# A dense network over pairwise products on one core: the last chunk's second layer as seven block products, and five smaller edits

## The reference

```python
interaction = jnp.einsum('bnd,bmd->bnm', bottom_output, bottom_output)
x = jnp.concatenate([bottom_mlp_output, interaction[:, _TRIL_R, _TRIL_C], zero_pad], axis=1)
x = jax.nn.relu(x @ W0.T + b0)
x = jax.nn.relu(x @ W1.T + b1)
x = jax.nn.relu(x @ W2.T + b2)
x = jax.nn.relu(x @ W3.T + b3)
return x @ W4.T + b4
```

## Time and profile before

| | us |
|---|---|
| median of 3 runs | 484.64 (484.17 to 485.58) |
| the profiled execution | 484.05 |
| its span, first to last instruction | 482.3 |
| PE busy | 470.3 |
| PEld busy | 399.2 |
| DVE busy | 282.8 |
| ACT busy | 242.6 |

### The profile page before, as it was taken

How to read it: one execution, slowest core, us unless ns; L and a number is a source line. 1 busy time by engine, 2 the same in 40 slices (tenths; PEclk the granted TensorE clock), 3 DMA queues, 4 the chain that set the end, 5 groups by cost and what they waited for, 6 DMA issues and landing times.

```text
span 482.3 us, 6717 instructions
## 1 busy us (share of the span) xinstructions
PE 470.3 (98%) x2495; PEld 399.2 (83%) x2495; DVE 282.8 (59%) x508; ACT 242.6 (50%) x580; POOL 0.7 (0%) x6
## 2 busy tenths in 40 slices
PE   8989999999997999999999999999999999999997
PEld 8979987878775888888888888888888888888885
DVE  4599779687765877575616877766624633110124
ACT  4996577758673366565653266665553321110112
POOL 0000000000000000000000000000000000000000
PEclk9999999999998999999999999999999999999999
DMA  8979555765273231843345141653224000434200
GB/s 306 379 253 390 175 163 187 253 218 190 87 270 139 85 101 39 307 150 134 103 183 212 44 141 37 219 222 130 87 96 167 1 0 1 175 101 161 87 1 1
DMA packets 18992, 72.28 MB, mean 150 GB/s; under 512 B 2448, under 2 KB 4496, under 8 KB 14864
## 3 DMA queue, kind: packets, MB, share of 16 engines
q1 hardware_dynamic: 18960, 71.86, 42.3%
HBM read 63.45 MB, written 8.40 MB: 149 GB/s over the span
## 4 chain that ended last, share of the span: by engine, by line
PE 82%; DVE 9%; DMA 4%; ACT 2%; issue 2%; SPq 0%; DVEq 0%; ACTq 0%
PE work L790 18%; PE work L792 17%; PE work L791 17%; PE gps L815 8%; PE acc L790 7%; PE acc L791 6%; PE acc L792 6%; DMA xraw<-x_t 4%; DVE turned L605 2%; ACT grams L416 1%; PE acc L912 1%; DVE turned L594 1%; PE gps L828 1%; DVE w1s L662 1%; DVE pairs L609 1%
## 5 line engine op out<-in xcount | busy, mean ns | idle before, releaser
L416 ACT ACTIVATE grams<-gps 32x216 f32<-32x216 f32 x384 | 131.5, 343 | 86.0 <-PE gps L815 82.5
L790 PE MATMUL work<-h1h,w1s 128*128 128x512 f32 x256 | 101.7, 397 | 0.5 <-DVE w1s L662 0.4
L792 PE MATMUL work<-h1l,w1s 128*128 128x512 f32 x256 | 100.4, 392 | 0.0
L791 PE MATMUL work<-h1h,w1s 128*128 128x512 f32 x256 | 100.2, 391 | 0.0
L448 ACT ACTIVATE act_out<-work,bias 128x512 f32<-128x512 f32 (+1 forms) x64 | 42.3, 662 | 90.9 <-PE work L792 89.6
L815 PEld LDWEIGHTS gps<-xs 128*128 128x128 f32 x384 | 56.6, 190 | 10.0 <-issue 1.4
L636 DVE CAST h2h<-act_out 128x512 fp32r<-128x512 f32 x40 | 17.0, 426 | 76.5 <-ACT act_out L448 76.5
L815 PE MATMUL gps<-xs 128*128 128x224 f32 x384 | 58.3, 274 | 0.4 <-DVE featL L627 0.3
L790 PE MATMUL work<-featH,w0l 126*128 126x512 f32 (+5 forms) x160 | 56.7, 354 | 1.1 <-ACT act_out L448 0.6
L792 PEld LDWEIGHTS work<-h1l,w1s 128*128 128x128 f32 x256 | 48.1, 188 | 10.6
L790 PEld LDWEIGHTS work<-h1h,w1s 128*128 128x128 f32 x256 | 48.3, 189 | 9.3 <-DVE w1s L662 1.4
(11 more groups left out here) (71 smaller groups left out, 520.5 us busy)
## 6 DMA issues: line engine op xcount, KB each, us to landing
xraw<-x_t SPq DMA_DIRECT2D x64, 432.0 KB, 4.2
w1s<-w_parts SPq DMA_DIRECT2D x24, 1024.0 KB, 4.8
w_parts<-w1s SPq DMA_DIRECT2D x8, 1024.0 KB, 4.8
stage<-w_t SPq DMA_DIRECT2D x8, 512.0 KB, 5.9
w0raw<-w_t SPq DMA_DIRECT2D x4, 512.0 KB, 8.0
w2raw<-w_t SPq DMA_DIRECT2D x4, 512.0 KB, 9.0
x0raw<-x_t SPq DMA_DIRECT2D x4, 256.0 KB, 5.3
w3raw<-w_t SPq DMA_DIRECT2D x1, 512.0 KB, 10.5
```

Of the source, the lines that this page charges most:

```text
L416: last = act.activation(grams2[rows, h // 2 % 2, at:at + HALF_GROUPS, :, :], src[:, :, :, q * EVEN:q * EVEN + INPUTS], ACT.Copy)
L790: pe.matmul(dst, wl, ah, start=start, stop=False)
L791: pe.matmul(dst, wh, ah, start=False, stop=False)
L792: return pe.matmul(dst, wh, al, start=False, stop=stop)
```

## The change

- **Layer 1 of the last chunk.** The weights and activations are cut in halves both ways, and tiles i and 4+i of the output (a "set", i from 0 to 3) come from seven block products P1 to P7 of 4 products each, 256 samples wide, in place of 16 products of 512 samples. ACT copies P1 out of PSUM, and DVE adds the blocks up in seven sums of 256 columns (U2, U4, C11, U3, C22, C21, C12); a block's bank is free for a later block once its sum is done. DVE also makes the operands: four sums of weights for each set (512 columns each, `s_sum`) with their parts (`s_hi_part` on ACT, `s_lo_part` on DVE, 1024 columns), and four differences of activations for each pair of layer 0 tiles (256 columns each, `t_sum`) with theirs (`t1_lo_part`, `t_lo_part`, `late_parts`). Set 0's weight sums stand at the end of chunk 2. Layer 0's tiles come in the order 0, 4, 1, 5, 2, 6, 3, 7.
- **Narrower grams.** The gram matmuls load 123 weight columns in place of 128.
- **Wide layer 4.** Weights are one column of `w4s`, the moving operand is 512 samples: 6 matmuls a chunk. DVE adds the bias to one row of 512, and each chunk's answers are stored by a DMA of their own.
- **Shifted opening.** Turns after slices 7, 11, 15; weight loads after slices 6, 8, 10, 12. Chunk 0's halves start at steps 2, 6, 10, 14, 19, so that half 5 stands at step 22, half 11 at 42, half 19 at 68, half 27 at 94, half 31 at 106, the turns at 40, 66, 92 and 117.
- **High parts from PSUM.** `relu` writes the high part straight from PSUM on ACT, ahead of `act_out`; DVE's cast is gone.

```diff
-        plans = [plan([3, 8, 13, 18, 23], 2, STEPS - 2)] + [plan([1], 3, STEPS - 6)] * (CHUNKS - 2) + [({}, {})]
+        plans = [plan([2, 6, 10, 14, 19], 2, STEPS - 3)] + [plan([1], 3, STEPS - 6)] * (CHUNKS - 2) + [({}, {})]
-        W0_AFTER = [5, 7, 8, 10]
+        W0_AFTER = [6, 8, 10, 12]
-        TRANSPOSE_AT = SLICES_SUB + 2
+        TRANSPOSE_AT = SLICES_SUB + 3
+        S_SUM_AT = {107: 0, 108: 1, 109: 2, 110: 3}
+        S_PART_AT = {110: 0, 111: 1}
...
+                act.activation(hi[:, kept_cols], bank[:, kept_cols], ACT.Relu, bias=bias[:, row:row + 1])\
+                   .then_inc(hi_done, 1)
                 act.activation(act_out[:, slot(layer, m, more), cols], bank[:, cols], ACT.Relu,
                                bias=bias[:, row:row + 1]).then_inc(relu_done, 1)
...
+                dve.wait_ge(hi_done, n + 1)
                 dve.wait_ge(relu_done, n + 1)
-                dve.tensor_copy(hi, full).then_inc(hi_done, 1)
-                dve.wait_ge(hi_done, n + 1)
                 dve.tensor_tensor(lo, full, hi.bitcast(f32), ALU.subtract).then_inc(split_done, 1)
...
+                def last_layers():
+                    for k in range(1, KQ):
+                        last_even(k)
+                        if k == 2:
+                            answers(c - 1)
+                            s_sum(1, 0)
+                            s_sum(1, 1)
+                        if k == KQ - 1:
+                            s_sum(1, 2)
+                            s_sum(1, 3)
+                        last_odd(k)
+                    for i in range(SETS):
...
+                        if i + 1 < SETS:
+                            s_lo_part(i + 1, 0)
+                        set_sum(i, "U2")
+                        set_sum(i, "U4")
+                        if i + 1 < SETS:
+                            s_lo_part(i + 1, 1)
+                        set_sum(i, "C11")
...
-                                     xs[:, p % XSLOTS, 0, four, :].rearrange("p b n -> p (b n)"),
+                                     xs[:, p % XSLOTS, 0, four, :].rearrange("p b n -> p (b n)")[:, 0:USED],
...
+            def block(i, name, weights, moving):
+                for k in range(KQ):
+                    last = product(place(name), *weights(k), *moving(k), k == 0, k == KQ - 1)
+                last.then_inc(block_done, 1)
...
+            def layers_last():
+                for i in range(SETS):
+                    p1(i)
+                    p5(i)
+                    if i:
+                        layer2_last(2 * i - 2)
+                    p6(i)
+                    p2(i)
+                    if 0 < i < SETS - 1:
+                        layer2_last(2 * i - 1)
+                    p7(i)
+                    p4(i)
+                    p3(i)
+                for pos in range(KT2 - 3, KT2):
+                    layer2_last(pos)
...
-                    for part, (h2, ready) in enumerate(((h2h, hi_done), (h2l, split_done))):
-                        pe.wait_ge(ready, n + 1)
-                        for s in range(SUBS):
-                            at = ((s * MT3 + k) * 2 + part) * 2
-                            last = pe.matmul(acc[:, 3, at:at + 2], h2[:, k, s * SUB:(s + 1) * SUB], w4s[:, k, :],
-                                             start=True, stop=True)
+                    n, whole = nth(c, 3, k, more), acc[0:1, 3, :]
+                    pe.wait_ge(hi_done, n + 1)
+                    pe.matmul(whole, w4s[:, k, 1:2], h2h[:, k, :], start=k == 0, stop=False)
+                    pe.matmul(whole, w4s[:, k, 0:1], h2h[:, k, :], start=False, stop=False)
+                    pe.wait_ge(split_done, n + 1)
+                    last = pe.matmul(whole, w4s[:, k, 0:1], h2l[:, k, :], start=False, stop=k == MT3 - 1)
```

More of the change, by code:

```diff
@@ L20 @@
 GCOLS = GROUP * EVEN
+USED = (GROUP - 1) * QUAD + INPUTS
 BANK = 512
@@ L42 @@
 TILES = MT0 + MT1 + MT2 + MT3
+SETS = MT1 // 2
+HALF = CHUNK // 2
+KQ = KT1 // 2
+WQ = KQ * P
+L0_ORDER = [t for i in range(SETS) for t in (i, SETS + i)]
+L1_ORDER = [t for i in range(SETS) for t in (SETS + i, i)]
+BLOCKS = ("P1", "P5", "P6", "P2", "P7", "P4", "P3")
+SUMS = ("U2", "U4", "C11", "U3", "C22", "C21", "C12")
 LOAD = 1024
@@ L172, in by_sample, with nth_block, nth_sum, place @@
             return buf[:, p % XSLOTS, :].rearrange("p (b n) -> p b n", n=INPUTS)
+        def nth_block(i, name):
+            return len(BLOCKS) * i + BLOCKS.index(name) + 1
+        def nth_sum(i, name):
+            return len(SUMS) * i + SUMS.index(name) + 1
+        def place(name):
+            bank = {"P1": gps[:, 0, :], "P7": gps[:, 0, :], "P5": work[:, 0, :], "P6": gps[:, 1, :], "P4": gps[:, 1, :],
+                    "P2": work[:, 1, :], "P3": work[:, 1, :]}[name]
+            return bank[:, 0:HALF]
+        def tiles(c, layer, m, more=True):
+            return nth(c, layer, m, more) + 1 - (MT1 if c == LAST and layer >= 2 else 0)
+        def tile0(c, m):
+            return L0_ORDER[m] if c == LAST else m
+        def split_columns(c, layer, m):
+            if c == LAST and layer == 0 and m % 2 == 0:
+                return LEFT
+            return columns(c) if layer == 0 else slice(0, CHUNK)
         def w0_piece(buf, n):
@@ L369, in body @@
                         load_x(c + 1, p)
+                if c == LAST:
+                    load_a22(0)
+                    load_raw(1)
+                    answer(c - 1)
+                    for i in range(2, SETS):
+                        load_raw(i)
+                        refill_set(i)
+                        load_a22(i - 1)
+                    load_a22(SETS - 1)
+                    return
+                if c == LAST - 1:
+                    load_raw(0)
                 for m in range(MT1):
+                    if c and m == 2:
+                        answer(c - 1)
                     if c == 0:
@@ L506, in on_tile @@
                 def on_tile(layer, m):
-                    relu(c, layer, m, work[:, m % 2, :])
+                    relu(c, layer, m, work[:, m % 2, :], h1h[:, tile0(c, m), :] if layer == 0 else h2h[:, m % 2, :])
                 def after_tile(m):
@@ new lines, in set_sum @@
+            def set_sum(i, name):
+                first, second = act_out[:, 1, :], act_out[:, 0, :]
+                left, right = slice(0, HALF), slice(HALF, CHUNK)
+                dst, block, part = {"U2": (U2, "P6", P1_OUT), "U4": (U4, "P5", U2), "C11": (first[:, left], "P2", P1_OUT),
+                                    "U3": (U3, "P7", U2), "C22": (second[:, right], "P5", U3),
+                                    "C21": (second[:, left], "P4", U3), "C12": (first[:, right], "P3", U4)}[name]
+                dve.wait_ge(block_done, nth_block(i, block))
+                if name == "U2":
+                    dve.wait_ge(copy_done, i + 1)
+                else:
+                    dve.wait_ge(sum_done, nth_sum(i, name) - 1)
+                dve.tensor_tensor(dst, place(block), part, ALU.add).then_inc(sum_done, 1)
@@ L949, in body @@
                         layer4(c - 1, True)
-                for m in range(MT1):
+                for m in range(MT1 if c < LAST else 0):
                     for k in range(KT1):
```

329 lines of the change are left out of this document (288 added, 41 removed).

## The result

The changed kernel takes 490.6 us (489.92 to 491.15) for 484.7 of the kernel before beside it: ratio 1.0122, 95% interval 1.0098 to 1.0147. It is slower, and 4.0 us outside the forecast range.

What follows compares the result with a forecast made beforehand. The prediction took TensorE as the bound almost everywhere. Its terms summed to -1.3 us, from 484.05 to 482.75, which goes to 483.3 against the median of 484.64; it wrote 483.4, range 480.0 to 486.6.

Steps and rivals of the forecast that it cites:

- a step costs 0.687: TensorE's price in us of one step, with 512-column matmuls starting 0.229 apart, taken from the earlier trace.
- 192 x 0.229: Last chunk's layers 1 and 2: 44.0 us of 512-column matmuls become 336 x 0.118 = 39.8, so -4.1.
- Rival 1: Clock falls in new waits at chunk 2's end and P1: 485.1 with one (chance 0.14), 486.8 with both (0.10).
- Opening: -1.8: Start of the kernel: shorter slice load and overlapping pieces bring the fourth transposes about 1.8 us earlier.
- The lower bound: Opening's gain was bounded between 0 and -2.6 us; the bound meant is 0, no gain.
- Chunk 0: Steps 0 to 23 +0.7 us, steps 24 to 115 +2.6, its end -4.5 with a wait of 0.8.
- my 1.85 and 1.25: Chunk 0: waits in us forecast at the first and second turn, with ACT and DVE behind.
- Grams: Gram matmuls: loads of 123 columns 0.1086 us apart in place of 0.113, -1.0 us, bounds 0 and 2.3.
- End of chunk 2: New wait of 2.6 us ahead of layer 2's last tile, behind four weight sums and two low parts.
- Last chunk's layers 1 and 2: +0.7 us: matmuls save 4.1, set 0 waits 4.8 (P1 2.45, P6 1.7, P3 0.6), sets 1 to 3 none.
- Layer 4 and the tail: Layer 4 -1.2 us, 0.4 in each of three chunks; tail +0.6, up to +1 if the store is dearer.
- the sum of -1.3: All terms together, opening to tail: -1.3 us, from 484.05 to 482.75.

Runs made afterwards that it cites:

- e5: Changed kernel with 96 more bytes ahead of TensorE's moving tiles, so they start 64 over a multiple of 128 as before: 486.75 us, ratio 1.0038.
- e2: Kernel before with 32 bytes left free ahead of xraw, putting moving tiles 96 bytes over a multiple of 128: 488.9 us, ratio 1.0086.
- e6: Kernel before with the shifted opening alone: its loads, transposes, VectorE order and half points: 485.5 us, ratio 1.0008.
- e8: e5 with the last chunk's preparations reordered, set 0's weight sums behind the first pair's low part: 480.3 us, ratio 0.9916.
- e12: e8 with the grams' loads 128 columns wide again in place of 123: 481.75 us, ratio 0.9928.
- e3: e1 with set 0's four weight sums moved from the end of chunk 2 into the last chunk, behind the first pair's low part: 484.2 us, ratio 0.9989.
- e11: e8 with layer 4, answers and store of the kernel before: 480.3 us, ratio 0.9899.
- e7: Kernel before with one edit, high parts made by a second ReLU on ScalarE in place of VectorE's cast: 486.7 us, ratio 1.0036.
- e1: Changed kernel with a 32-byte pad that puts the moving tiles at a multiple of 128: 487.4 us, ratio 1.0044.
- e4: Kernel before with weights 32 bytes over a multiple of 128 and moving tiles at a multiple: 487.8 us, ratio 1.0053.

## Why the prediction was wrong, point by point

- **The step that failed is the price of a matmul.** "a step costs 0.687" and "192 x 0.229" took the pitch from the earlier trace rows into a layout in which it is 3.1 to 4.1 ns more in layer 1. I looked at what the diff does to queues and never at where its new tiles push the old ones. The missing term is +4.1 us (e5 against after; e2, from the other side, has 4.2); less it the measured time would be 486.5, at the very edge of the range, the other misses below making up the rest.
- **Rival 1 came true once**: the fall at 375.0 behind a wait of 2.4. In the sum that is +1.7. P1's 2.1 brought none. With the missing term alone, rival 1's 485.1 becomes 489.2.
- **Opening: -1.8 was 0.** The left half began 1.5 us sooner, but the fourth transposes on VectorE did not come earlier with it: they start at 39.59 for 39.62, and the splits of the left half stand behind them. So TensorE waits 0.94 and 0.30 at 42.6 and 46.5, and step 0 is at 52.61 for 52.63. The lower bound that I had written down held; e6 confirms it.
- **Chunk 0**: steps 0 to 23 +1.4 for +1.2, and step 24 on -1.7 for -2.5, of which 0.3 is the place (e8, without a fall too, has 86.2 for 86.5). The waits of 1.33 and 1.80 behind the first and second turn answer to my 1.85 and 1.25. At the end of the chunk the wait is 0.62 and the clock 1.00, as forecast, but the sum of the chunk's waits is unchanged (5.9 for 5.8), and that the clock did not fall behind the 1.80 is partly luck: e5's did.
- **Grams: right in size.** 0.6 to 1.5 us between e8 and e12 for 1.0. Loads are 106 to 107 ns apart for 108.6, but those of 128 columns were 109.3 and not 113 in chunks 1 and 2: only 0.8 us stand in the grams themselves, and the rest in the matmuls right behind each half, which the term did not have.
- **End of chunk 2: right** in place, releaser and nearly size, 2.4 for 2.6 (e3 and e8 remove it by moving the sums that I named).
- **Last chunk's layers 1 and 2: right.** -1.9 for -1.8; P1 2.1, P6 1.4 and P3 none for 2.45, 1.7 and 0.6; sets 1 to 3 without waits. The seven products are worth what was said; e8 shows that the cost of set 0 was one of order alone.
- **Layer 4 and the tail**: -0.3 a chunk for -0.4, and the tail +1.5 for +0.6, since the answers' single row takes 1.10 us and not 0.69, and the last matmul waits 0.9 for a low part that ends later. e11, with both undone, takes the same time as e8.

Of the 7.2 us between the sum of -1.3 and the 5.9 measured, 4.1 are the place, 1.7 the clock, 1.8 the opening, 0.9 the tail; the shorter waits at the end of chunk 2 and at P1, P6 and P3 took back 1.5. That is 7.0, as near as a term of 4.1 known to 1.6 allows.

## What to carry to other kernels

When a change adds or resizes a buffer, compare the start addresses of TensorE's operands before and after, and keep stationary and moving tiles at the same place against 128 bytes; 32 bytes were worth 4 us of 485 here. A wait that is priced right can often be moved for nothing: write down what is queued ahead of the instruction that ends it, and try that in another order before judging the change. When a wait is gone from its place, add up the waits of the whole stretch before calling it a gain: here it went from the end of chunk 0 to its turns, and e6 and e7, the two parts alone, are no faster either.

## What the runs showed of the hardware

- The start of a 512-column fp32r matmul follows the one before it by 226.8 to 234.2 ns, by the places of its two operands; VectorE's and ScalarE's use of SBUF moved it by no more than 0.2 ns. In the kernels the first such matmul behind a gram half is followed at 237 to 241 ns on the mean. With 256 columns it is 117.8 to 119.9. The Trainium skill, TensorE: Matmul & The Clock Gate, Back-to-back issue gap, gives 216 by its formula for an isolated matmul, whatever the places; the runs have 5 to 8% more, and a spread that it doesn't tell of.
- The clock fell to the 1.2 GHz level behind or in idle times (bracket) of 1.80 and 2.31 (e5), 2.07 (e7), 2.15 (e6), 2.22 (after), 2.39 (e1), 2.54 (before) and 2.95 us (e3), and stayed at the 2.4 GHz level behind 1.80 (e8), 1.90 (after, P1), 2.03 (e1, P1), 2.46 (e2) and 2.47 (e4). The length of the wait doesn't tell it alone; a wait of 1.8 to 2.5 us has to carry both prices. Each fall lasted 3.4 us. Nor is the number of falls a property of the kernel: of 29 executions of the kernel before beside e5, six had a mean clock of 0.999 or 1.000 and took 482.4 to 484.1 us, twelve 0.992 or 0.993 and took 485.0 to 486.8. So a fall, or its absence, in one profile is one draw, and differences of a few us are told by medians of many executions.
- An operation of VectorE on one row of 512 from PSUM, read and written in different orders, took 1.10 us, for the 0.69 of a subtraction of 512 columns on 128 rows between SBUF tiles. Which of the differences counts was not tried.
